# Second attention of a two-layer block: heads on 32-row tiles, query chunks outermost, experts inside the loop

## What is computed

```python
x = x + attn(layernorm(x))          # 16 heads of 64, position table added to the keys, out projection
h = layernorm(x)                    # (1, 2048, 128)
# the second layer, on h; 16 heads of 8
q, k, v = h @ Wq + bq, h @ Wk + bk, h @ Wv + bv        # each (2048, 16, 8)
a = softmax(q @ k.T * 8 ** -0.5) @ v                    # per head, 2048 queries over 2048 keys
s = layer_norm(h + a @ Wo + bo, ln1_g, ln1_b)
e = remainder(floor(s @ router_w + router_b), 4)        # one of 4 experts per token
ff = relu(s @ W1[e] + b1[e]) @ W2[e] + b2[e]            # 128 -> 512 -> 128
x = x + layer_norm(s + ff, ln2_g, ln2_b)
```

## Time and profile before

| | |
|---|---|
| median of 3 runs | 2565.23 us (2563.91 to 2567.64) |
| the profiled execution | 2564.11 us, span 2562.1 us, so 2.0 us lie outside the span |
| mean granted clock of TensorE | 0.970 of full speed |
| busy: PE, DVE, ACT, POOL | 2419.0 (94%), 1973.2 (77%), 1140.1 (44%), 1024.6 (40%) |
| first attention | from the start to about 1447 us |
| norm, projections, first maximum passes | 1447.2 to 1529.9 us |
| main loop of the second attention | 1529.9 to 2394 us |
| what is behind it | 2394 to 2562.1 us |

### The profile page before, as it was taken

One profiled execution on the slowest core, in us unless ns is written; L12 is line 12 of the kernel. 1 busy time (PEld: TensorE's weight loads), 2 busy tenths in 40 slices (PEclk: granted clock), 3 DMA queues, 4 the chain that ended last, 5 costly groups with the idle time before them and its releaser, 6 DMA issues. The chain is left out here.

```text
span 2562.1 us, 37776 instructions
## 1 busy us (share of the span) xinstructions
PE 2419.0 (94%) x13217; PEld 1301.3 (51%) x13217; DVE 1973.2 (77%) x3173; ACT 1140.1 (44%) x1210; POOL 1024.6 (40%) x459
## 2 busy tenths in 40 slices
PE   5999999999999999999999599999998999999696
PEld 3455555555555555555555254555454455445465
DVE  5777777877777777777776598888887988888834
ACT  0344444444444444444444205565655556655332
POOL 1676777777868777768676400000000000000000
PEclk8999999999999999999999759999999999999898
DMA  2000000000000000000000000000000000000000
GB/s 84 1 1 1 1 1 1 1 1 1 1 1 1 1 1 1 1 1 1 1 1 1 21 4 5 12 5 5 5 8 9 7 8 5 5 7 10 17 0 16
DMA packets 17398, 16.61 MB, mean 6 GB/s; under 512 B 4656, under 2 KB 13760, under 8 KB 17088
## 3 DMA queue, kind: packets, MB, share of 16 engines
q1 hardware_dynamic: 17216, 14.20, 2.1%
HBM read 8.16 MB, written 1.05 MB: 4 GB/s over the span
## 5 line engine op out<-in xcount | busy, mean ns | idle before, releaser
L808 POOL TENSOR_TENSOR accp<-accp,prob 128x1024 f32<-128x1024 f32 x320 | 787.8, 2462 | 97.3 <-ACT prob L722 64.9
L722 ACT ACTIVATE prob<-scores 128x1024 f32<-128x1024 f32 x512 | 524.0, 1025 | 618.2 <-PE scores L409 569.4
L992 DVE TENSOR_REDUCE mxp<-ring 128x1 f32<-128x512 f32 x1024 | 637.0, 681 | 203.5 <-PE ring L384 203.5
L753 ACT ACTIVATE prob<-scores 128x1024 f32<-128x1024 f32 x512 | 496.6, 1022 | 416.4 <-PE scores L568 416.4
L421 PE MATMUL acc_o<-prob,v 128*64 128x512 f32 x2048 | 495.7, 605 | 0.0
L532 PE MATMUL ring<-khi,klo_q 128*128 128x512 f32 x1104 | 449.3, 451 | 9.8 <-DVE accs L1141 3.7
L1118 DVE TENSOR_REDUCE mxp<-ring 128x1 f32<-128x512 f32 x576 | 372.1, 686 | 37.6 <-PE ring L532 37.3
L1118 DVE TENSOR_REDUCE accs<-ring 128x1 f32<-128x512 f32 x528 | 343.6, 687 | 50.9 <-PE ring L532 50.4
L532 PEld LDWEIGHTS ring<-khi,klo_q 128*128 128x128 f32 x1104 | 214.0, 195 | 311.0 <-DVE mxp L1118 133.4
L404 PE MATMUL scores<-klo_q,khi 64*128 64x512 f32 x2048 | 354.6, 418 | 0.0
L568 PE MATMUL scores<-klo_q,khi 128*128 128x512 f32 x1028 | 338.8, 411 | 6.8 <-issue 6.6
(11 more groups left out here) (119 smaller groups left out, 1474.0 us busy)
## 6 DMA issues: line engine op xcount, KB each, us to landing
klo_q<-stage_q SPq DMA_DIRECT2D x72, 64.0 KB, 2.0
w_all<-w_pairs SPq DMA_DIRECT2D x1, 1344.0 KB, 11.2
klo_q<-m_rows SPq DMA_DIRECT2D x68, 2.0 KB
pos_sb<-pos SPq DMA_DIRECT2D x1, 1024.0 KB, 5.7
mrow<-m_rows SPq DMA_DIRECT2D x64, 2.0 KB
v<-w SPq DMA_DIRECT2D x1, 1024.0 KB, 5.3
prob<-w SPq DMA_DIRECT2D x4, 256.0 KB, 3.7
out<-prob SPq DMA_DIRECT2D x4, 256.0 KB, 2.4
```

The costliest lines, as they stand in the source:

```text
L722: nc.scalar.activation(prob[:, T % SLOTS1, :, :], sc[T % 2][:, :, :], ACT.Exp, scale=SCALE1).then_inc(exp_done, 1)
L753: nc.scalar.activation(prob2[:, u, t % 4, :, :], sc[u][:, :, :], ACT.Exp, scale=SCALE2).then_inc(exp2_done[u], 1)
L808: nc.gpsimd.tensor_tensor(accp[:, k % 2], accp[:, k % 2], prob[:, T % SLOTS1], ALU.add).then_inc(pool_acc, 1)
L992: done(nc.vector.reduce_max(mxp1[k % 2][:, h * QT + q, kc:kc + 1], bank[:], AX.X), ("max", k, q, kc, h))
```

## The change

**Tiles.** `q4` with its zero rows is gone. Queries of a block lie in `q_all[:, n % 4]`, keys of all four groups in `k_all[:, g]`, and a head's matmul reads only its 32 rows (`quarter(h)`), for scores and maxima alike. Values stay as they were, but the projections of all groups are done at once, per 512 tokens, before or in block 0.

**Order.** Query chunks are outermost, groups innermost. A chunk is then complete after four blocks, and its out projection, norm, router and experts become items of the ring in the blocks of the next chunk (`items2`, `experts`). Only the last chunk's follow the loop (`end2`). The loop is written out, without a hardware loop.

**A step.** Two of the four maximum tiles (heads 2 and 3) come between the two pairs of scores, the other two (heads 0 and 1) behind the values.

**Splits.** VectorE adds only the bias to a projection (`plus_bias`); GpSimd does the rounding split in two passes (`split2`). The maxima's row goes into `q_all` directly, by four DMAs as before; the DMAs that moved queries are gone. `prob2` has two slots per pair of heads in place of four.

**Norms.** GpSimd computes the reciprocal deviation for a chunk with six small operations, a power and a correction (`deviations`), and for chunks 0 to 2 the normalisation and the experts' bias rows too (`normalised3`, `expert_rows`, `normalised4`). In the last chunk VectorE normalises.

The core of the diff:

```diff
-TILES2 = [(h, q, k) for h in range(4) for q in range(QT) for k in range(NC)]
+def tiles2(n, t):
+    to = n + 1 if t < MAX2_STEPS else n + 2
+    q, kc = divmod((t + EARLY2) % STEPS2, NC)
+    if to >= BLOCKS2:
+        return [], []
+    return [(to, h, q, kc) for h in (2, 3)], [(to, h, q, kc) for h in (0, 1)]
+
+def experts(c):
+    items = [("h", c, 0, f) for f in range(FT)]
+    for e in range(E):
+        for q in range(QT):
+            items.append(("yo", c, e, q))
+            if e + 1 < E:
+                items.append(("h", c, e + 1, q))
+    return items
+
+FF_STEPS = (2, 4, 5, 6, 7, 8, 9, 10, 11, 13, 14)
+
+def items2(n, t):
+    c, g = divmod(n, GROUPS)
+    items = []
+    if n < 2:
+        if n == 0 and t in (1, 3, 6):
+            items.append(("V2", {1: 1, 3: 2, 6: 3}[t]))
+        if t in (5, 7, 8, 9):
+            items.append(("K2", n + 2, (5, 7, 8, 9).index(t)))
+    if t == 1 and n > 0:
+        items.append(("o", n - 1))
+    if t == 4 and n + 2 < BLOCKS2:
+        items.append(("Q2", n + 2))
+    if t == MAX2_STEPS and n + 1 < BLOCKS2:
+        items.append(("fin2", n + 1))
+    if c > 0:
+        if g == 0:
+            items += {5: [("ot", c - 1)], 7: [("wo", c - 1)], 14: [("xt", c - 1)], 15: [("rk", c - 1)]}.get(t, [])
+        elif t in FF_STEPS:
+            k = FF_STEPS.index(t) + len(FF_STEPS) * (g - 1)
+            items += experts(c - 1)[k:k + 1]
+    return items
...
-                nc.tensor.matmul(bank[:], q4[:, c, h, q * 128:(q + 1) * 128], k4[:, par, k * CW:(k + 1) * CW],
-                                 start=True, stop=True).then_inc(side_full, 1)
+                end(nc.tensor.matmul(bank[:], q_all[quarter(h), n % 4, q * 128:(q + 1) * 128],
+                                     k_all[quarter(h), n % GROUPS, kc * CW:(kc + 1) * CW], start=True, stop=True),
+                    ("max2", n, h, q, kc))
...
+            for n in range(BLOCKS2):
+                for t in range(STEPS2):
+                    T = STEPS2 * n + t
+                    for u, couple2 in enumerate(tiles2(n, t)):
+                        if T + 1 < STEPS2 * BLOCKS2:
+                            scores2(T + 1, u)
+                        if u == 0:
+                            for x in couple2:
+                                max2(*x)
+                    values2(T)
+                    for x in couple2:
+                        max2(*x)
+                    for it in items2(n, t):
+                        item2(it)
+            for it in end2():
+                item2(it)
...
+            def split2(key, to, part, n, ready, count):
+                wait_free(pool, key)
+                if n > 0:
+                    pool.wait_ge(rounded_ready, n)
+                nc.gpsimd.tensor_scalar(rounded[:], kf[:], parts_sb[:, part:part + 1], None, ALU.mult).then_inc(rounded_ready, 1)
+                pool.wait_ge(rounded_ready, n + 1)
+                nc.gpsimd.tensor_tensor(to, kf[:], rounded[:].bitcast(F32), ALU.subtract).then_inc(ready, 1)
```

More of the change, by code:

```diff
@@ new lines, in end2, with uses2 @@
+def end2():
+    c = NC - 1
+    return [("o", BLOCKS2 - 1), ("ot", c), ("wo", c), ("xt", c), ("rk", c)] + experts(c)
+def uses2():
+    uses = start2()
+    for n in range(BLOCKS2):
+        for t in range(STEPS2):
+            for couple in tiles2(n, t):
+                uses += [("max2", *x) for x in couple]
+            uses += items2(n, t)
+    return uses + end2()
+USES = uses1() + uses2()
+USE = {key: n for n, key in enumerate(USES)}
+assert len(USE) == len(USES)
+assert all(("h", c, e, f) in USE and ("yo", c, e, f) in USE for c in range(NC) for e in range(E) for f in range(FT))
@@ L509, in transposes @@
-            def transposes(norm, src):
-                pe.wait_ge(tokens_ready, norm)
-                for c in range(NC):
-                    bank = side()
-                    for q in range(QT):
-                        last = nc.tensor.transpose(bank[:, q * 128:(q + 1) * 128], src[:, c * QT + q, :], ident[:])
-                    last.then_inc(side_full, 1)
-            def proj(par, col, src_lo):
-                bank = side()
-                nc.tensor.matmul(bank[:], w_sb[:, par, col * 128:(col + 1) * 128], xnt[:, src_lo:src_lo + CW],
-                                 start=True, stop=True).then_inc(side_full, 1)
@@ L648, in _, with quarter, tokens2 @@
-            rebase(START3, START3 % RING)
-            pe.wait_ge(ld3, 16 * LOADS3)
-            pe.wait_ge(side_free, START3)
-            for c in range(NC):
-                bank = side()
+            rows2()
+            def quarter(h):
+                return slice(32 * h, 32 * h + 32)
+            def tokens2(c):
+                pe.wait_ge(s_ready, c + 1)
+                bank = begin(("T2", c))
+                for q in range(QT):
+                    last = nc.tensor.transpose(bank[:, q * 128:(q + 1) * 128], s_sb[:, c * QT + q, :], ident[:])
+                end(last, ("T2", c))
@@ L656, in _, with o_proj @@
-            for c in range(NC):
-                bank = side()
-                pe.wait_ge(side_free, START3 + c + 1)
+                end(last, ("ot", c))
+            def o_proj(c):
+                wait_free(pe, ("ot", c))
+                bank = begin(("wo", c))
+                for q in range(QT):
+                    last = nc.tensor.matmul(bank[:, q * 128:(q + 1) * 128], ot[:, c % 2, q * 128:(q + 1) * 128], wo_sb[:],
+                                            start=True, stop=True)
+                end(last, ("wo", c))
@@ L659, in _, with x_turn, router @@
+            def x_turn(c):
+                pe.wait_ge(x_ready, c + 1)
+                bank = begin(("xt", c))
+                for q in range(QT):
+                    last = nc.tensor.transpose(bank[:, q * 128:(q + 1) * 128], s_sb[:, c * QT + q, :], ident[:])
+                end(last, ("xt", c))
+            def router(c):
+                wait_free(pe, ("xt", c))
+                bank = begin(("rk", c))
                 for q in range(QT):
                     t = c * QT + q
-                    last = nc.tensor.matmul(bank[:, q * 128:(q + 1) * 128], ot[:, t * 128:(t + 1) * 128], wo_sb[:],
-                                            start=True, stop=True)
@@ L686, in _, with hidden @@
-            with pe.Fori(0, NC) as c:
-                hidden(c, 0)
-                for e in range(E):
-                    if e < E - 1:
-                        hidden(c, e + 1)
-                    expert_out(c, e)
+                    last = nc.tensor.matmul(bank[:, q:q + 1], xnt[:, t * 128:(t + 1) * 128], rw_sb[:], start=True, stop=True)
+                end(last, ("rk", c))
+            def hidden(c, e, f):
+                wait_free(pe, ("xt", c))
+                pe.wait_ge(w1_ld, 16)
+                bank = begin(("h", c, e, f))
+                end(nc.tensor.matmul(bank[:], w1_sb[:, e, f * 128:(f + 1) * 128], xnt[:, c * CW:(c + 1) * CW],
+                                     start=True, stop=True), ("h", c, e, f))
@@ L923, in _ @@
+            store(NC - 2)
+            store(NC - 1)
+            for a in range(2):
+                sp.wait_ge(out_dma[a], 16 * NC // 2)
         @block.vector
```

1001 lines of the change are left out of this document (494 added, 507 removed).

## The result

The changed kernel takes 2534.14 us (median of four runs, 2525.10 to 2536.38), the kernel before 2566.11 on the same chip: a ratio of 0.9869, 95% interval [0.9844, 0.9895]. So it is faster by 1.3%, but of the 128 us that I expected to gain only 32 came. The time lies outside the main forecast's own range, 2395 to 2480; the wide range, 2360 to 2575, holds it by luck, since it went that far up for dear items, which are not what happened. The profiled execution took 2534.56 us with a span of 2532.5.

What follows compares the result with a forecast made beforehand. TensorE was taken to bound the main loop before the change, the ring's circle after it. 1529.9 us up to the loop, 841 of loop and 63 behind it, plus 2.0 outside the span, gave 2436 us; own range 2395 to 2480, wide 2360 to 2575.

Steps and rivals of the forecast that it cites:

- dear items: Rival for the main loop: each item costs 1.2 us instead of 0.60, +89 us, 2525 us; chance 0.12.
- Plain step, 2.92 us: Main loop: a step without an item lasts 2.92 us, against 3.03 before; 236 such steps make 689 us.
- the circle: Main loop: waits through the three-bank ring, from head 0's tile behind the values to the next step's, 2.92 us.
- Tiles side by side: Main loop: 32-row matmuls on different rows overlap, so a pair takes the 0.23 us of a single one.
- the rival without overlap: Main loop: 32-row tiles don't overlap, 3.15 us a step, +54 us, 2490 us; chance 0.11.
- VectorE alone (2.4 us): Rival for the main loop: VectorE alone bounds the step, 2.4 us, -123 us, 2313 us; chance 0.10.
- An item, 0.60 us: Main loop: an item delays the step by one reduction, 0.60 us; 148 of them make 89 us.
- By that rule the clock stays up and the 2436 stands: TensorE's clock in the loop: without long idle gaps between bursts it stays up, leaving the forecast at 2436 us.
- the rival's 0.15: Chance 0.15 that the loop's clock falls and stays down: 4.50 us a step, 2809 us, or 2622 with half slow.
- a clock of 0.5 over tens of steps: Sign in the loop that would make the forecast wrong: granted clock 0.5 over tens of steps, where 1.00 was forecast.
- Between the attentions, 0: Stage between the two attentions, 82.7 us before: no change in time, between -10 and +15 us.
- Behind the loop, 63: Stage behind the main loop: only chunk 3 is left, 63 us against 168.1, between 50 and 85.

## Why the prediction was right and wrong

- **Plain step, 2.92 us: right.** 2.98 at 2.4 GHz, and moving head 3's tile took the 0.23 us out that the circle gives to the scores of head 3. The difference is in the signal: head 0's reduction starts at 1685.73 and takes 0.69, and head 3's tile starts at 1686.57, so 0.15 us lie between where I took 0.05.
- **Tiles side by side: right.** A score of head 2 and a tile of head 3 both start at 1686.57. In the row-tile-less kernel the step is 3.22, close to the 3.15 of the rival without overlap.
- **VectorE alone (2.4 us): did not come.** It idles 0.50 us a step, as forecast. The Trainium skill ("TensorEngine Tiling (Array Packing)", "PSUM Bottleneck") says that with TensorE faster the copy out of PSUM may become the bottleneck, no more than "may"; here VectorE's reading is in the circle, but 2.75 us was reached with VectorE's work unchanged, and 2.4 in no run.
- **An item, 0.60 us: right.** Steps with one take 3.58 us. With the clock's loss taken out the loop would be 852 us, forecast 841.
- **The clock: here the prediction failed.** The step "By that rule the clock stays up and the 2436 stands", with the rival's 0.15 as its only trace in the numbers. The price of a slow step was right (4.62 for 4.50). What I held against the fall, "the values alone keep 0.86 us unbroken in each step", was no protection. And the case that came, some 40 slow steps costing 68 us, was in no term: I had the clock up, or down in half or all of the steps. The sign that I named myself, a clock of 0.5 over tens of steps, came. The tile pass of the earlier trace rows, at 1.2 GHz with a matmul every 0.60 us, was the right row to look at, but I read from it only how dense the stream is. Its matmuls were full-width ones. That narrow tiles weaken the clock even where TensorE never stops was not thought of, and it is what the kernel before with row tiles showed.
- **The Trainium skill's rule** ("TensorE: Matmul & The Clock Gate", "Why this matters for your kernels"), no long idle gaps between bursts, does not decide this case: the loop at 0.50 for 1227.9 us had TensorE busy for 1217.77 of them. My doubt of the rule was right, but the sum was made as if it held.
- **Between the attentions, 0: came out at +8.6**, inside my -10 to +15. Part of it is in the place named, the projections that wait for each other's split:

```profile
1466.14 1.58 POOL L868 TENSOR_SCALAR rounded<-kf,parts_sb 128x512 fp32r<-128x512 f32 x1 [5.65 <-DVE kf L1220]
1467.80 1.26 POOL L870 TENSOR_TENSOR k_all<-kf,rounded 128x512 fp32r<-128x512 f32 x1
1469.17 0.75 DVE L1220 TENSOR_SCALAR kf<-ring,bqk_sb 128x512 f32<-128x512 f32 x1 [3.21 <-POOL k_all L870]
...
1484.97 0.75 DVE L1220 TENSOR_SCALAR kf<-ring,bqk_sb 128x512 f32<-128x512 f32 x1 [1.16 <-PE ring L523]
```

  The split's first pass takes 1.58 us, not the 1.26 of the row that I took for both, so VectorE waits 3.1 to 3.2 us, four times, where I had 2.6. Five more times it waits 1.16 us for a projection on TensorE, at 1.2 GHz, which stood in no term. How the 8.6 us divide stays open, since the forecast for this stage was not added up from terms; spreading the projections took away only 2 of them.
- **Behind the loop, 63: 74.5.** Two terms were too small. The experts' bias rows, "16 passes over 128x128 at perhaps 0.35", 12 us in all, took 15.1, from 2478.46 to 2493.61: a pass is 0.59 (2.34 / 4). The products behind them, 24 us in the sum, took 29.6, from 2493.61 to 2523.2: at each of the three changes of expert TensorE waits 0.98 us for ScalarE's ReLU, and the first pairs of products ran at 1.2 GHz, after TensorE had stood still for 9.15 us:

```profile
2478.46 2.36 POOL L909 TENSOR_SCALAR own_row<-tail_rows,mask 128x128 f32<-128x128 f32 x4 [9.11 <-DVE mask L1284]
...
2486.04 2.34 POOL L909 TENSOR_SCALAR own_row<-tail_rows,mask 128x128 f32<-128x128 f32 x4
...
2493.61 0.61 DVE L1294 SCALAR_TENSOR_TENSOR ff<-ring,mask,ff 128x128 f32<-128x128 f32 x2 [15.26 <-POOL ff L911]
2494.10 2.04 PE L618 MATMUL ring<-xnt,w_all 128*128 128x512 f32 x2 [9.15 <-DVE ff L1294]
```

  Another 4 us lie ahead of the rows, and the last norm and store took 0.7 less than their 10. That the rows on VectorE gave back 10.6 us is not the miss made good: most of it is time that the forecast had granted to GpSimd.

Sum of the misses: 8.6 + 78.5 + 11.5 = 98.6, which is, but for rounding, the span's 2532.5 less the 2434 of the forecast. 68 of them are the clock.

## What to carry to other kernels

When matmuls are cut to fewer rows, or TensorE comes to wait, take the granted clock as a term of the sum with its own price, and count the steps at each level in the new trace before any other explanation is tried. If steps are slow and TensorE has slack in the circle that sets the step, a full-width matmul whose result is thrown away is one added line and tells at once what the clock costs; where TensorE has no slack, row tiles can lose more than they save. For a step held by a ring of buffers, write down the circle and look which instructions stand behind the blocked one without need: moving one matmul gave 0.23 us a step.

## What was not expected of the hardware

- TensorE can be at 1.2 GHz for a whole loop while it is busy 99% of it: 255 steps in a row with 32-row scores and maxima, where the same instructions on 128 rows had a granted clock of 0.99.
- Of matmuls added in idle time, one over 128 rows left 2 slow steps, two of 32 rows left 11 side by side and 13 in a row, none left 36.
- The time of such a kernel moves from one execution to the next: 2530 to 2619 us with one tile behind the values, 11 us of spread with one full-width matmul added to each of its steps (2460.50 to 2471.64).
- A change between 32-row and full-width matmuls costs TensorE time of its own: 0.72 us from start to start at 1.2 GHz instead of 0.43, and 0.43 at 2.4 GHz instead of 0.23.
- GpSimd's rounding pass over 128x512 takes 1.56 to 1.58 us, its subtraction 1.26, a multiplication of 128x128 by a column 0.59.

Not settled: what exactly the chip looks at when it grants the clock, why the falls come just behind short items, and why the old order needs more full-width work for it than the new one.
